# GpSimd's multiplication of the state by C without its wait for the next inject (one layer: GCN, Mamba scan, mixture of experts)

## The chip, the cores and the metric

The kernel runs on one core of a Trainium2 chip. The metric is the device time of one execution in microseconds (us); lower is better. The core has five engines with a queue each: TensorE (PE in the rows; its weight loads are PEld), VectorE (DVE), ScalarE (ACT), GpSimd (POOL) and SyncE (SP), which only issues DMAs here. They run their queues in order and wait for each other on semaphores.

## The reference, cut to what matters

The input x has 8192 rows of 128 values, and adj is a dense 8192 x 8192 matrix. The layer first adds a graph convolution followed by a Mamba block, and then a top-1 mixture of 8 experts.

```python
h = relu(adj @ layernorm(x) @ gcn_w + gcn_b);  h = layernorm(h)
xz = h @ w_in;  xc, z = xz[:, :256], xz[:, 256:]
u = silu(causal_conv4(xc));  dbc = u @ w_xp
dt = softplus(dbc[:, :8] @ w_dt + b_dt);  B = dbc[:, 8:24];  C = dbc[:, 24:]
dA = exp(dt[:, :, None] * A);  dBu = dt[:, :, None] * B[:, None, :] * u[:, :, None]
hst = dA[t] * hst + dBu[t];  ys[t] = hst @ C[t]          # over t, hst is 256 x 16
x = x + ((ys + u * D_skip) * silu(z)) @ w_out
H = gelu(layernorm(x) @ W1 + b1);  p = softmax(H @ Wg + bg);  e = argmax(p)
x = x + p[e] * (H @ Wd[e] + bd[e])
```

The part that the change touches is the sum over the 16 states in `hst @ C[t]`. For each state the kernel makes dA (`decay`), dBu (`inject`), the scan over time (`hidden`), the product with C (`h_c`), and adds that to `y_sum`.

## The kernel before

The 8192 rows are cut into 16 tiles of 512. `body(i)` is a software pipeline, written for every engine: it multiplies the adjacency of tile i+2 (`adjacency`), runs convolution, normalisation, projections and dt of tile i+1 (`front`), the 16 states of tile i (`mamba`), the output product and gating of tile i-1 (`ffn`), the scatter of the rows of tile i-2 to the experts' bins, and a batch of expert work of older tiles (`batch`, `late`). Within a body every engine loops over `s`, the state, from 0 to 15, and all other work is hung into the slot of some s by hand. Nothing but this written order and the semaphores sets what runs when. The data of one state is a 128 x 1024 float32 block: 256 channels as two halves of 128 partitions, 512 time steps each.

What VectorE does in slot s, in order:

- the scan of state s in two halves (line 779). It reads `decay` in SBUF and `inject` in PSUM and writes `hidden[:, s % 2]`.
- in some slots, work of the other stages. Slots 0, 1, 12 and 14 have chains of small instructions; slot 3 has a sum from PSUM and statistics (lines 811 to 819), slot 4 has two products (823, 827), slots 11 and 13 two PSUM reads each (834, 839), slot 7 six convolution steps (872, after the sum below), and slot 15 a cast, four PSUM reads and a product (760, 763, 909).
- the sum `y_sum += h_c` of state s-1 (line 863; lines 848 and 856 are its forms in slots 0 and 1). Both of its inputs are in SBUF. It waits for GpSimd's h_c of state s-1.
- the product `inject = dtu * B` of state s+1 (line 916). Both of its inputs, `dtu_sb` and a row of `bc_ring`, are in SBUF; its output goes to PSUM.

GpSimd makes `h_c[:, s % 2] = hidden[:, s % 2] * C` of state s in one instruction (line 440), both inputs and the output in SBUF, and then issues the indirect DMAs of that slot, which scatter rows, gather rows and weights, or write output (lines 401, 406, 411, 447). ScalarE makes `decay` of state s+1 and keeps the last column of the scan. SyncE loads `bc_ring`, a ring of four states' B and C, and the adjacency ring; its load of state t waits for h_c of state t-4, and later adjacency loads stand behind it on the same queue.

Before h_c of state s, GpSimd waits for three things: the scan of s, the sum of s-2 (it frees `h_c[:, s % 2]`), and `inject` of the next state. `next_state` yields the next state of this tile, after state 15 the first one of the next tile, and nothing where there is no next tile. Nothing in h_c's data depends on that inject.

Of the kernel before, what the change touches and what calls it, by code (L numbers as in the profile page):

```python
# [39 lines left out]
def gnn_mamba_moe(nc, x_rows, x_cols, adj, vecs, consts, sel, gcn_w, w_in, w_xp, w_dt, w_out, W1, Wg, Wd, bd, out):  # L40
# [12 lines left out]
    with ExitStack() as ctx:  # L53
# [131 lines left out]
        def over_halves(ap):  # L185
            return ap.unsqueeze(1).broadcast_to([P, 2, T])
# [19 lines left out]
        def sem(name, per=1):  # L206
            s = ctx.enter_context(nc.semaphore(name))
            PER[name] = per
            return s
# [23 lines left out]
        decay_ready, inject_ready, scan_ready = (  # L233
            sem("decay_ready", SLOTS), sem("inject_ready", SLOTS), sem("scan_ready", SLOTS))
# [55 lines left out]
        def bodies(eng, body):  # L290
            for i in range(-2, 6):
                body(i, i % 2, **stages(i))
            with eng.Fori(6, TILES - 3, 2) as i:
                body(i, 0, **ALL)
                body(i + 1, 1, **ALL)
            for i in range(TILES - 2, TILES + 2):
                body(i, i % 2, **stages(i))
# [4 lines left out]
        def next_state(s, mamba, front):  # L302

            if s + 1 < SLOTS:
                return ((0, s + 1),) if mamba else ()
            return ((1, 0),) if front else ()
# [72 lines left out]
        @block.gpsimd  # L379
        def _(pool):  # L380
            def constant(dst, pattern, base, lanes):
                nc.gpsimd.iota(dst, pattern, base=base, channel_multiplier=lanes,
                               allow_small_or_imprecise_dtypes=True).then_inc(start_c, 1)

            constant(lane[:], [[0, 1]], 0, 1)
            constant(lane8[:], [[0, 1]], 0, EXPERTS)
            constant(need[:], [[0, 1]], EXPERTS, EXPERTS)
            constant(full_at[:], [[0, EXPERTS], [EXPERTS * P, PICKS]], EXPERTS * P, 0)
            constant(some_at[:], [[0, EXPERTS], [EXPERTS * P, PICKS]], EXPERTS, 0)
            constant(offset[:], [[0, EXPERTS], [EXPERTS * P, PICKS]], 0, 0)  # L390
            constant(owner[:], [[P, EXPERTS], [0, PICKS]], 0, 0)
            constant(turn[:], [[1, PICKS], [0, EXPERTS * PICKS]], 1, 0)
            constant(head[:], [[1, EXPERTS]], 0, 0)
            constant(bt_sb[:, 0:P], [[1, P]], 0, 0)
            for q in range(2):
                constant(id_col[:, q], [[P, BLOCKS]], q * T - 2 * T, 1)
            pool.wait_ge(start_v, 1)
            constant(got[0:1, 0, 0, REC - 1:REC], [[0, 1]], 1 << 30, 0)

            def gather_weights(r, j):  # L400
                nc.gpsimd.indirect_dma_start(  # L401
                    out=wd_ring[:, r, j].rearrange("p k c -> p (k c)"), out_offset=None, in_=wd_rows.ap(),
                    in_offset=bass.IndirectOffsetOnAxis(ap=wd_at[:, r, j:j + 1], axis=0)).then_inc(wd_in[r], 16)

            def gather_rows(r, j):
                nc.gpsimd.indirect_dma_start(  # L406
                    out=got[:, r, j], out_offset=None, in_=bins.ap(),
                    in_offset=bass.IndirectOffsetOnAxis(ap=row_at[:, r, j:j + 1], axis=0)).then_inc(row_in[r], 16)

            def scatter_out(r, j):  # L410
                nc.gpsimd.indirect_dma_start(  # L411
                    out=out, out_offset=bass.IndirectOffsetOnAxis(ap=out_at[:, r, j:j + 1], axis=0),
                    in_=o_sb[:, r, j], in_offset=None, bounds_check=N - 1, oob_is_err=False).then_inc(out_in[r], 16)

            def body(i, p, adjacency, front, mamba, ffn, scatter, batch, late):
                c = Count(pool, i)
                q = 1 - p
                for per in (1, 4, 5, 6, 16, 64):
                    c.times_of(per)
                for s in range(SLOTS):  # L420
                    if late and s in OUT_SLOTS:
                        c.wait(o_ready, -5, PICKS + 1)
                    if scatter and s == 1:
                        pool.wait_ge(zero_in, 16 + 16 * FILLS)
                        c.wait(dest_step, -2, 6)
                        c.wait(xn_ready, -2, BLOCKS)
                        c.wait(id_step, -2, 1)
                    if batch and s == 5:
                        pool.wait_ge(table_in, 16 * 2 * EXPERTS)
                        c.wait(ctrl_step, -4, 16)  # L430
                        c.wait(by_done, -6, PICKS)
                    if batch and s == 6:
                        c.wait(scat_in, -2, 16 * BLOCKS)
                        c.wait(o_ready, -6, PICKS + 1)
                    if mamba:
                        c.wait(scan_ready, 0, s + 1)
                        for d, t in next_state(s, mamba, front):
                            c.wait(inject_ready, d, t + 1)
                        c.wait(y_step, 0, s - 1)
                        nc.gpsimd.tensor_tensor(h_c[:, s % 2], hidden[:, s % 2],  # L440
                                                over_halves(bc_ring[:, s % BC_RING, 1]), ALU.mult
                                                ).then_inc(hc_ready, 1)
                    if late and s in OUT_SLOTS:
                        scatter_out(q, OUT_SLOTS.index(s))
                    if scatter and s in (1, 2, 3, 4):
                        b = s - 1
                        nc.gpsimd.indirect_dma_start(  # L447
                            out=bins.ap(), out_offset=bass.IndirectOffsetOnAxis(ap=dest[:, b:b + 1], axis=0),
                            in_=rec[:, p, b], in_offset=None).then_inc(scat_in, 16)
                    if batch and s in (5, 8, 9):  # L450
                        for j in {5: (0, 1), 8: (2,), 9: (3,)}[s]:
                            gather_weights(p, j)
                    if batch and s in (6, 7):
                        for j in (2 * (s - 6), 2 * (s - 6) + 1):
                            gather_rows(p, j)

            bodies(pool, body)
            for f in range(FLUSH):
                k = BATCHES + f
                c = Count(pool, k)  # L460
                c.wait(o_ready, -2, PICKS + 1)
                pool.wait_ge(flush_step, 23 * f + 23)
                c.wait(by_done, -2, PICKS)
                if f == 0:
                    pool.wait_ge(scat_in, 16 * BLOCKS * TILES)
                for j in range(PICKS):
                    gather_rows(k % 2, j)
                for j in range(PICKS):
                    gather_weights(k % 2, j)
                if f:  # L470
                    c.wait(o_ready, -1, PICKS + 1)
                    for j in range(PICKS):
                        scatter_out((k - 1) % 2, j)
            c.wait(o_ready, 0, PICKS + 1)
            for j in range(PICKS):
                scatter_out(k % 2, j)
# [674 lines left out]
```

## Time and profile before

| | us |
|---|---|
| three runs before | 1887.21, 1882.68, 1887.48 |
| median | 1887.21 |
| the profiled execution, its own time | 1887.13 |
| its span, first to last instruction | 1885.3 |
| first scan starts, last h_c starts | 158.2, 1715.4 |

So 1.8 us lie outside the span. The states fill the middle 1557 us, some 97 us for a tile. Ahead of them x is normalised and the first two tiles of the adjacency are multiplied; behind them the experts' remaining batches run. A busy time is the time in which an engine executes; the profile also says, for idle time ahead of an instruction, what ended it. A line in a row is the line of the kernel above.

### The profile page before, as it was taken

To read this page: it belongs to the slowest core of one execution; us is meant where nothing else is said; L and a number is where in the kernel's file an instruction comes from. 1 tells how busy PE (TensorE), PEld (TensorE's weight loads), DVE (VectorE), ACT (ScalarE), POOL (GpSimd) and SP (SyncE) were. 2 spreads that over 40 slices of the span, in tenths; PEclk is the share of its full clock that TensorE was granted. 3 is DMA by queue.
4 is the path that set the end of the run, shared out by engine and by line. 5 is a ranking of instruction groups with operands and counts; after the bars stand their busy time and mean duration, and the time that the engine had idled before them with its cause. 6 is when DMAs were issued, how large, how long until landed. Compare 5 with 4: busy or idle time off the path is not lost. (4 is left out here: it accounts for less than half of the span.)

```text
span 1885.3 us, 18148 instructions
## 1 busy us (share of the span) xinstructions
PE 1534.3 (81%) x4568; PEld 770.3 (41%) x4568; DVE 1557.7 (83%) x2103; ACT 846.2 (45%) x1500; POOL 978.9 (52%) x553
## 2 busy tenths in 40 slices
PE   6799888898989898998989898999899866345554
PEld 2343334444434444444435353544444433223342
DVE  8016999999998999999898989999989999996221
ACT  2033445454446373645464544546363645444211
POOL 0002443545455574747474756666574747586444
PEclk9899998999998999998988999999989886656777
DMA  8899997978776878787787878788868754242232
GB/s 302 296 311 391 379 347 276 328 264 313 260 287 232 307 269 307 261 310 281 274 284 273 283 272 285 270 285 283 270 238 311 260 178 139 94 146 79 82 99 50
DMA packets 155792, 479.52 MB, mean 254 GB/s; under 512 B 19477, under 2 KB 45602, under 8 KB 155698
## 3 DMA queue, kind: packets, MB, share of 16 engines
q1 hardware_dynamic: 139954, 428.59, 64.7%
q0 software_dynamic: 14592, 45.77, 7.5%
q10 hardware_dynamic: 1152, 4.19, 0.6%
q14 instruction: 71, 0.58, 0.1%
q8 instruction: 23, 0.38, 0.1%
HBM read 447.88 MB, written 33.75 MB: 255 GB/s over the span
## 5 line engine op out<-in xcount | busy, mean ns | idle before, releaser
L987 PE MATMUL ps_adj<-ring,nodes 128*128 128x512 f32 x2048 | 964.0, 619 | 86.0 <-DMA ring<-adj 53.5
L440 POOL TENSOR_TENSOR h_c<-hidden,bc_ring 128x1024 f32<-128x1024 f32 x256 | 601.8, 2351 | 783.6 <-DVE inject L916 706.7
L779 DVE TENSOR_TENSOR_SCAN hidden<-decay,state,inject 128x512 f32<-128x512 f32 x512 | 627.6, 1268 | 54.0 <-ACT decay L524 22.9
L987 PEld LDWEIGHTS ps_adj<-ring,nodes 128*128 128x128 f32 x2048 | 397.7, 199 | 610.2 <-issue 481.7
L524 ACT ACTIVATE decay<-dt_sb,negA 128x512 f32<-128x512 f32 x512 | 339.4, 711 | 1.2 <-DVE dt_sb L839 1.0
L916 DVE TENSOR_TENSOR inject<-dtu_sb,bc_ring 128x1024 f32<-128x1024 f32 x256 | 314.4, 1228 | 22.1 <-DMA bc_ring<-bc_dram 14.8
L863 DVE TENSOR_TENSOR y_sum<-y_sum,h_c 128x1024 f32<-128x1024 f32 x224 | 273.5, 1221 | 23.1 <-POOL h_c L440 21.7
L517 ACT COPY state<-hidden 128x2 f32<-128x2 f32 x256 | 49.4, 193 | 535.3 <-DVE hidden L779 534.8
L411 POOL DMA_INDIRECT out<-o_sb,out_at x72 | 85.2, 1183 | 68.3 <-DVE dest L795 22.4
L401 POOL DMA_INDIRECT wd_ring<-wd_rows,wd_at x72 | 105.3, 1462 | 16.6 <-issue 13.6
L406 POOL DMA_INDIRECT got<-bins,row_at x72 | 92.2, 1280 | 18.3 <-issue 16.5
L447 POOL DMA_INDIRECT bins<-rec,dest x64 | 92.6, 1446 | 11.5 <-issue 6.0
L938 PE MATMUL ps_e<-bt_sb,w_sb 128*128 128x512 f32 x128 | 88.0, 825 | 2.3 <-ACT H L629 1.2
L938 PE MATMUL ps_e<-wd_ring,H 128*128 128x128 f32 x512 | 74.1, 292 | 14.7 <-ACT H L629 14.0
L938 PE MATMUL ps_y<-const_sb,rec 128*128 128x128 f32 x128 | 25.1, 357 | 70.1 <-ACT rec L558 70.1
L938 PEld LDWEIGHTS ps_y<-wg_sb,H 128*128 128x128 f32 x512 | 76.6, 240 | 11.0 <-issue 11.0
L938 PE MATMUL ps_f<-u_sb,wxp_sb 128*128 128x512 f32 x64 | 42.1, 793 | 46.4 <-ACT H L597 44.4
L938 PEld LDWEIGHTS ps_e<-wd_ring,H 128*128 128x128 f32 x512 | 69.0, 207 | 22.8 <-ACT H L629 16.5
L938 PE MATMUL ps_y<-wg_sb,H 128*128 128x8 f32 x512 | 77.8, 293 | 0.0
L872 DVE SCALAR_TENSOR_TENSOR u_sb<-conv_in,vec_sb,u_sb 128x512 f32<-128x512 f32 x96 | 65.0, 746 | 11.6 <-ACT u_sb L577 11.6
L938 PE MATMUL ps_e<-const_sb,got 128*128 128x128 f32 x128 | 22.3, 327 | 61.0 <-DMA got<-bins,row_at 59.9
L938 PE MATMUL ps_f<-front_a,win_sb 128*128 128x512 f32 x128 | 69.9, 674 | 0.8 <-ACT conv_in L570 0.8
(166 smaller groups left out, 1360.6 us busy)
## 6 DMA issues: line engine op xcount, KB each, us to landing
ring<-adj SPq DMA_DIRECT2D x512, 512.0 KB, 5.6
bc_ring<-bc_dram SPq DMA_DIRECT2D x256, 512.0 KB, 5.7
bins<-nodes SPq DMA_DIRECT2D x96, 172.0 KB
nodes<-x_rows ACTq DMA_DIRECT2D x8, 512.0 KB, 12.2
x_tile<-x_rows SPq DMA_DIRECT2D x16, 256.0 KB, 5.3
wd_rows<-Wd SPq DMA_DIRECT2D x8, 256.0 KB, 5.0
wd_ring<-wd_rows,wd_at POOLq DMA_INDIRECT x72, 6.3
got<-bins,row_at POOLq DMA_INDIRECT x72, 3.8
```

Source lines behind the costliest of these rows:

```text
L401: nc.gpsimd.indirect_dma_start(out=wd_ring[:, r, j].rearrange("p k c -> p (k c)"), out_offset=None, in_=wd_rows.ap(), in_offset=bass.Indir ...
L406: nc.gpsimd.indirect_dma_start(out=got[:, r, j], out_offset=None, in_=bins.ap(), in_offset=bass.IndirectOffsetOnAxis(ap=row_at[:, r, j:j + ...
L411: nc.gpsimd.indirect_dma_start(out=out, out_offset=bass.IndirectOffsetOnAxis(ap=out_at[:, r, j:j + 1], axis=0), in_=o_sb[:, r, j], in_offs ...
L440: nc.gpsimd.tensor_tensor(h_c[:, s % 2], hidden[:, s % 2], over_halves(bc_ring[:, s % BC_RING, 1]), ALU.mult).then_inc(hc_ready, 1)
L447: nc.gpsimd.indirect_dma_start(out=bins.ap(), out_offset=bass.IndirectOffsetOnAxis(ap=dest[:, b:b + 1], axis=0), in_=rec[:, p, b], in_offs ...
L524: exp = nc.scalar.activation(decay[:, t % 2, h], dt_sb[:, p if d == 0 else q, h], ACT.Exp, scale=negA[:, h, t:t + 1])
L779: scan = nc.vector.tensor_tensor_scan(hidden[:, s % 2, h], decay[:, s % 2, h], inject[:, h], state[:, h, s:s + 1], ALU.mult, ALU.add)
L863: nc.vector.tensor_tensor(y_sum[:], y_sum[:], h_c[:, (s - 1) % 2], ALU.add).then_inc(y_step, 1)
L872: nc.vector.scalar_tensor_tensor(out=u_sb[:, h], in0=conv_in[:, h, k:k + T], scalar=vec("conv_w", TAPS * h + k), in1=u_sb[:, h], op0=ALU.m ...
L916: nc.vector.tensor_tensor(inject[:], dtu_sb[:], over_halves(bc_ring[:, t % BC_RING, 0]), ALU.mult).then_inc(inject_ready, 1)
L938: last = nc.tensor.matmul(dst, stationary, moving, start=(n == 0), stop=(n == len(pairs) - 1))
L987: last = nc.tensor.matmul(ps_adj[:, 0], nodes[:, m], ring[:, g % RING, m % GROUP], start=(m == 0), stop=(m == J - 1))
```

## The change

The two lines that make GpSimd wait for the next inject are taken out. No instruction is added, removed or moved on any engine; lines behind the edit move up by two.

```diff
                     if mamba:
                         c.wait(scan_ready, 0, s + 1)
-                        for d, t in next_state(s, mamba, front):
-                            c.wait(inject_ready, d, t + 1)
                         c.wait(y_step, 0, s - 1)
                         nc.gpsimd.tensor_tensor(h_c[:, s % 2], hidden[:, s % 2],
```

## Rows read from the trace of the kernel before

**Rows 1.** The page, part 1: busy time, share of the span, instructions.

```profile
PE 1534.3 (81%) x4568; PEld 770.3 (41%) x4568; DVE 1557.7 (83%) x2103; ACT 846.2 (45%) x1500; POOL 978.9 (52%) x553
```

**Rows 2.** Busy time in two stretches: length, PE, PEld, DVE, ACT, POOL, granted clock, DMA.

```profile
923.00:1025.00 102.00, 92.56 (x274) 46.89 (x272) 93.61 (x125) 51.03 (x91) 59.30 (x33) 0.90 0.78 269
...
1628.00:1716.00 88.00, 33.85 (x128) 25.08 (x128) 83.16 (x107) 36.24 (x67) 64.72 (x33) 0.60 0.34 111
```

**Rows 3.** The page, part 5: busy us, mean ns, idle before, its releaser.

```profile
L440 POOL TENSOR_TENSOR h_c<-hidden,bc_ring 128x1024 f32<-128x1024 f32 x256 | 601.8, 2351 | 783.6 <-DVE inject L916 706.7
...
L916 DVE TENSOR_TENSOR inject<-dtu_sb,bc_ring 128x1024 f32<-128x1024 f32 x256 | 314.4, 1228 | 22.1 <-DMA bc_ring<-bc_dram 14.8
L863 DVE TENSOR_TENSOR y_sum<-y_sum,h_c 128x1024 f32<-128x1024 f32 x224 | 273.5, 1221 | 23.1 <-POOL h_c L440 21.7
```

**Rows 4.** Timeline, one ordinary state (start us, us, engine): DVE and POOL.

```profile
584.48 2.45 DVE L779 TENSOR_TENSOR_SCAN hidden<-decay,state,inject 128x512 f32<-128x512 f32 x2
584.53 2.34 POOL L440 TENSOR_TENSOR h_c<-hidden,bc_ring 128x1024 f32<-128x1024 f32 x1 [0.42 <-issue]
...
586.90 1.23 DVE L863 TENSOR_TENSOR y_sum<-y_sum,h_c 128x1024 f32<-128x1024 f32 x1
...
588.05 1.23 DVE L916 TENSOR_TENSOR inject<-dtu_sb,bc_ring 128x1024 f32<-128x1024 f32 x1
...
589.41 2.35 POOL L440 TENSOR_TENSOR h_c<-hidden,bc_ring 128x1024 f32<-128x1024 f32 x1 [0.41 <-DVE inject L916]
```

**Rows 5.** Timeline, the last state of the last tile: DVE, then POOL.

```profile
1712.89 2.45 DVE L779 TENSOR_TENSOR_SCAN hidden<-decay,state,inject 128x512 f32<-128x512 f32 x2
1715.31 1.23 DVE L863 TENSOR_TENSOR y_sum<-y_sum,h_c 128x1024 f32<-128x1024 f32 x1
1716.45 2.31 DVE L760 CAST out_at<-got 128x4 uint32<-128x4 f32 x1
1718.67 1.11 DVE L763 SCALAR_TENSOR_TENSOR o_sb<-ps_e,got 128x128 f32<-128x128 f32 x4
```

```profile
1715.42 3.31 POOL L440 TENSOR_TENSOR h_c<-hidden,bc_ring 128x1024 f32<-128x1024 f32 x1
```

**Rows 6.** Queries by line and tile: duration ns as min/median/max, first and last start.

```profile
L440 POOL TENSOR_TENSOR h_c<-hidden,bc_ring x256: 2328/2346/3307, 163.0 to 1715.4; 128x1024 f32<-128x1024 f32 x128
```

```profile
L760 DVE CAST out_at<-got x18: 159/164/2305, 621.3 to 1862.8; 128x4 uint32<-128x4 f32 x18
```

```profile
L779 DVE TENSOR_TENSOR_SCAN hidden<-decay,state,inject x512: 1252/1268/1282, 158.2 to 1714.1; 128x512 f32<-128x512 f32 x171
```

**Rows 7.** Timeline of DVE in one tile: slots 3, 4, 11 and 12.

```profile
841.90 2.45 DVE L779 TENSOR_TENSOR_SCAN hidden<-decay,state,inject 128x512 f32<-128x512 f32 x2
...
846.24 1.19 DVE L863 TENSOR_TENSOR y_sum<-y_sum,h_c 128x1024 f32<-128x1024 f32 x1
...
848.67 2.45 DVE L779 TENSOR_TENSOR_SCAN hidden<-decay,state,inject 128x512 f32<-128x512 f32 x2
...
851.69 1.22 DVE L863 TENSOR_TENSOR y_sum<-y_sum,h_c 128x1024 f32<-128x1024 f32 x1
...
889.01 2.45 DVE L779 TENSOR_TENSOR_SCAN hidden<-decay,state,inject 128x512 f32<-128x512 f32 x2
...
892.68 1.22 DVE L863 TENSOR_TENSOR y_sum<-y_sum,h_c 128x1024 f32<-128x1024 f32 x1
...
898.65 0.18 DVE L879 TENSOR_TENSOR logit<-ps_y,vec_sb 128x32 f32<-128x32 f32 x1
898.87 0.19 DVE L883 TENSOR_REDUCE top<-logit 128x4 f32<-128x32 f32 x1
```

**Rows 8.** Waits: us in total, times, longest.

```profile
DVE hidden L779 <- ACT decay L524: 22.9, 10, 5.0
...
DVE inject L916 <- issue: 5.5, 6, 1.9
DVE hidden L779 <- POOL h_c L440: 5.1, 2, 2.6
```

```profile
SPq L362 <- POOL h_c L440: 490.9, 134, 8.5
```

## The prediction

> **What bounds the kernel now.** I read the busy shares first, then single stretches, then the timeline of one state. Over the whole span VectorE is busy 83% and TensorE 81% [rows 1]; the average hides that the kernel has three parts. In the middle part, where the 16 states of 16 tiles run, VectorE works 93.61 of 102 us and GpSimd 59.30 [rows 2]; most of VectorE's small gaps are the short hand-over ahead of a scan. TensorE is busy 92.56 us there too, and in the last tile, with no adjacency left, only 33.85 of 88 us, while VectorE still works 83.16 of them [rows 2]. So VectorE's own queue sets the pace of the states, with TensorE close behind, and what adds a microsecond between two scans adds it to the end.
>
> Then one state [rows 4]: two scans take 2.45 us, the sum y_sum 1.23, the inject 1.23, and the next scans start; this is a period of 4.9 us without slack. GpSimd's h_c (2.34 us) starts with the scans of the next state, at 584.53, and is over 0.03 us before y_sum starts at 586.90. So h_c always runs under the scans, and never beside y_sum or inject. The change ends exactly this: h_c of state s becomes free to start when scan s ends, which is when VectorE goes on to y_sum and inject.
>
> GpSimd's idle time ahead of h_c is large, 783.6 us, of which 706.7 were ended by inject [rows 3]. It is no cost by itself: GpSimd isn't the bound. What VectorE loses to GpSimd is the wait of y_sum for h_c, 21.7 us in all [rows 3], plus 5.1 us of scans put down to h_c [rows 8]. That is all that an earlier h_c can give back directly.
>
> **What an early h_c costs.** The trace of before holds one instance of the changed kernel. Behind the last state of the last tile there is no next inject, so h_c waited only for its scan [rows 5]. The scans end at 1715.34; y_sum starts at 1715.31 and h_c at 1715.42. y_sum keeps its 1.23 us and ends at 1716.54. h_c takes 3.31 us instead of the median 2.346 [rows 5, 6]: it stood still until y_sum was over and then ran, 1716.54 to 1718.73. VectorE's next instruction, a cast of 128x4 values, took 2305 ns where its median is 164 [rows 6]: it began before y_sum had ended and yet finished only with h_c. So the two engines exclude each other here, the one that is ahead goes first, and at the hand-over GpSimd wins against a VectorE instruction that is already queued. The price for VectorE is 2305 - 164 = 2.14 us.
>
> Which instructions take part? The scans don't: all 512 lie between 1252 and 1282 ns although nearly all run beside h_c [rows 6], and they read one SBUF tensor, write SBUF and take inject from PSUM. y_sum reads two SBUF tensors and did hold up h_c. Inject reads two as well. That inject will itself be held up by a running h_c is my inference, since the held instruction of the trace is a cast with one input. The Trainium skill says it outright (SBUF — State Buffer, Who interferes with whom): a VectorE instruction with two SBUF inputs and a GpSimd instruction that reads SBUF exclude each other for the whole instruction, and whichever issues first goes first. The trace agrees for y_sum against h_c (3.31 us for 2.35); for inject against h_c no row of before shows it.
>
> **The sum, slot by slot of a full tile.** No queue is reordered and no DMA moved; only the start of h_c, and with it the indirect DMAs behind it, come earlier by up to one y_sum and one inject.
> - Slots 2, 5 to 10, 14 and 15 have y_sum straight behind the scans. y_sum goes first, h_c next, and the instruction after y_sum (inject, the convolution, a small product or the cast) is held 2.14 us. Slots 0 and 1 have chains of small instructions ahead of y_sum, some with two SBUF inputs; h_c is ready 0.08 us behind the scan's end and takes over after the first of them, for about the same 2.14. These are 11 slots, 23.5 us.
> - In slot 3 the work ahead of y_sum reads PSUM or one tensor and can run beside h_c. h_c would run from 0.08 to 2.43 us behind the scan's end, and y_sum used to start at 846.24 - 844.35 = 1.89 [rows 7]: held 0.5 us, or 0.9 if the small tensor_scalar there is held; I take 0.8. Slot 4: y_sum used to start 851.69 - 851.12 = 0.57 behind the scan; held 1.7 to 1.9, I take 1.7. Slot 11: 892.68 - 891.46 = 1.22, held 1.2; slot 13 has the same shape, 1.2. In slot 12 the two instructions behind y_sum (0.18 and 0.19 us) have at most one SBUF tensor and a vector, and run beside h_c [rows 7]: 2.14 less 0.37, 1.8.
> - Together 23.5 + 0.8 + 1.7 + 1.2 + 1.2 + 1.8 = 30.2 us a tile, and 16 x 30.2 = 483 us.
>
> Against it stands what goes. y_sum's waits for h_c, 21.7 us, vanish, since h_c of s-1 is over before scan s. VectorE's waits for others shrink as VectorE itself becomes later: 22.9 us of scans on decay, 5.5 us of inject behind the logits, 5.1 us on h_c, 33.5 us in all [rows 8]. TensorE has some 92 us of work for a tile that now lasts about 127, so I let all of these go. SyncE's queue waits 490.9 us for h_c [rows 8], with adjacency loads behind it; it will wait longer, but in step with VectorE, so it costs TensorE time it no longer needs.
>
> The profiled execution took 1887.13 us, as good as the median of 1887.21. 1887.1 + 483 - 21.7 - 33.5 = 2315 us.
>
> **Its own range.** Low end: if only instructions over 0.5 us are held and the small chains run beside h_c, slots 0, 1, 14 and 15 lose 0.6 to 1.6 us of their price each, about 4 us a tile, 65 us in all: 2250. If h_c also sometimes falls under waits that stay, some 20 less, 2230. High end: the other waits stay (+33), and each of the 11 hits costs a whole h_c of 2.35 instead of 2.14 (+37): 2385; a TensorE whose granted clock sinks as it idles more (0.60 in the last tile against 0.90 [rows 2]) could lengthen the chains through TensorE and ScalarE: 2400. Below nothing the cost can't go in this case, since VectorE is the bound in every tile and 483 us is twenty times what is given back.
>
> **The rivals.**
> - *Inject keeps the port* (no change). y_sum and inject are back to back and of one kind, while the trace's held instruction was a cast. If VectorE passes from one to the other without letting go, h_c stands still through both and then runs under the next scans, exactly as before. The sum is the old one: h_c of about 4.8 us, 1887 us, within 0.3%. For it: two instructions of VectorE overlap in the rows by some 0.09 us. Against it: the cast overlapped y_sum by the same 0.09 (1716.45 against 1716.54) and lost.
> - *No exclusion of inject, and the gain comes* (faster). If only y_sum holds up h_c, and inject, which writes PSUM, runs beside it, then h_c is over 2.35 us behind y_sum, well before the next y_sum. y_sum's 21.7 us and the scans' 5.1 go: 1887.1 - 26.8 = 1860; TensorE, nearly as busy, would take a part of it back, so 1865. It decides itself on whether inject stays at 1228 ns with h_c beside it. Against it: y_sum and inject have the same kinds of inputs, and the held cast has fewer.
> - *Held in some slots only.* Who wins at y_sum's end may turn on a few tens of ns and come out differently in even and odd bodies. Half of the hits would give about 2090; 1900 to 2230.
> - *The wait was idle.* That the change does nothing because h_c waits for something else is excluded: 706.7 us of idle time end with inject [rows 3].
>
> **How the numbers follow.** The full hold-up has 0.76, the port kept by inject 0.08, the gain 0.06, some slots only 0.08, above 2400 us 0.02. The forecast is 2315 us. 2230 to 2400 holds the first case; down to 2120 it takes in about half of the partial one, near 0.8 in all. About 0.3% is what a measurement of this kernel can tell from no change: faster by more 0.06, within 0.08, slower by more 0.76 + 0.08 + 0.02 = 0.86.
>
> **What would show it.** Inject's mean rises from 1228 to about 2.9 to 3.4 us, h_c's from 2351 to some 3.2, while y_sum stays near 1221 and the scans at 1268. VectorE's busy time rises by about 450 us, as held time counts as busy. An ordinary state takes 7.0 us from scan to scan instead of 4.9, a tile about 127 us, and y_sum's wait for h_c is gone. Inject at 1228 ns with h_c in y_sum's shadow would make the prediction wrong on its second step; h_c at 4.8 us would prove the first rival.

## The result and the profile after

The changed kernel takes 2306.43 us (median of four runs, 2304.65 to 2309.28) against 1886.7 us (median of four runs of the kernel before); the ratio is 1.2229, 95% interval 1.2204 to 1.2254. It is slower by 420 us. The profiled execution took 2304.65 us, its span is 2302.8.

The page of the changed kernel, parts 1 and 5 (busy us, mean ns, idle before, releaser; lines behind the edit are two lower than in the rows of before):

```profile
PE 1598.0 (69%) x4568; PEld 803.1 (35%) x4568; DVE 2023.7 (88%) x2103; ACT 848.0 (37%) x1500; POOL 1121.2 (49%) x553
...
L438 POOL TENSOR_TENSOR h_c<-hidden,bc_ring 128x1024 f32<-128x1024 f32 x256 | 749.1, 2926 | 1059.3 <-DVE hidden L777 1045.6
...
L777 DVE TENSOR_TENSOR_SCAN hidden<-decay,state,inject 128x512 f32<-128x512 f32 x512 | 627.6, 1267 | 33.4 <-issue 9.8
...
L914 DVE TENSOR_TENSOR inject<-dtu_sb,bc_ring 128x1024 f32<-128x1024 f32 x256 | 537.1, 2098 | 16.5 <-DMA bc_ring<-bc_dram 14.7
...
L861 DVE TENSOR_TENSOR y_sum<-y_sum,h_c 128x1024 f32<-128x1024 f32 x224 | 328.2, 1465 | 0.0
```

The number of instructions is that of [rows 1], but VectorE is busy 2023.7 us where it was 1557.7: 466.0 us more for the same work. Its idle time in the span fell from 327.6 to 279.1 us. The two together are the 417.5 us between the spans. Against [rows 3], inject grew from 1228 to 2098 ns on average, y_sum from 1221 to 1465, h_c from 2351 to 2926; the scans kept their 1267. y_sum waits for h_c no longer.

One ordinary state (slot 5) in the timeline, first VectorE, then GpSimd:

```profile
1054.24 1.20 DVE L861 TENSOR_TENSOR y_sum<-y_sum,h_c 128x1024 f32<-128x1024 f32 x1
1055.36 3.38 DVE L914 TENSOR_TENSOR inject<-dtu_sb,bc_ring 128x1024 f32<-128x1024 f32 x1
1058.84 2.45 DVE L777 TENSOR_TENSOR_SCAN hidden<-decay,state,inject 128x512 f32<-128x512 f32 x2
```

```profile
1054.42 3.24 POOL L438 TENSOR_TENSOR h_c<-hidden,bc_ring 128x1024 f32<-128x1024 f32 x1 [2.89 <-DVE hidden L777]
1057.81 1.81 POOL L401 DMA_INDIRECT wd_ring<-wd_rows,wd_at  x1 [0.15 <-issue]
1059.93 0.96 POOL L401 DMA_INDIRECT wd_ring<-wd_rows,wd_at  x1 [0.30 <-issue]
```

This is [rows 5] repeated: y_sum is first, h_c stands until it ends at 1055.44 and runs to 1057.66, and inject, queued at 1055.36, ends 1.08 us behind h_c. Where other work stands behind the scans, another instruction is hit. VectorE in slots 0, 1, 3, 4 and 11 of the same tile:

```profile
1014.30 1.99 DVE L793 CAST dest<-dest_f 128x4 uint32<-128x4 f32 x1
...
1022.74 2.40 DVE L699 TENSOR_TENSOR has<-rem,full_at 128x32 f32<-128x32 f32 x1
...
1041.12 0.93 DVE L815 TENSOR_SCALAR rec<-rec 128x4 f32<-128x4 f32 x1
...
1047.69 2.95 DVE L861 TENSOR_TENSOR y_sum<-y_sum,h_c 128x1024 f32<-128x1024 f32 x1
...
1101.20 2.30 DVE L861 TENSOR_TENSOR y_sum<-y_sum,h_c 128x1024 f32<-128x1024 f32 x1
```

Instructions of some 0.2 us take 2 us because h_c is running: the product `has` (2.40 us for 0.19) with two inputs in SBUF, but also two instructions with one, the cast in slot 0 and the tensor_scalar at 1041.12 (0.93 us for 0.17). In every slot of every tile one instruction is held.

### The profile page after: what moved, and what is told of

The parts are those of the page before. It is cut to its first block and busy times, and to the rows that moved or that the text cites. A ratio compares the mean times of both kernels' runs of the same rounds, so it can differ in the third digit from the quotient of the medians.

```text
span 2302.8 us, 18078 instructions
## 1 busy us (share of the span) xinstructions
PE 1598.0 (69%) x4568; PEld 803.1 (35%) x4568; DVE 2023.7 (88%) x2103; ACT 848.0 (37%) x1500; POOL 1121.2 (49%) x553
## 5 line engine op out<-in xcount | busy, mean ns | idle before, releaser
L438 POOL TENSOR_TENSOR h_c<-hidden,bc_ring 128x1024 f32<-128x1024 f32 x256 | 749.1, 2926 | 1059.3 <-DVE hidden L777 1045.6
L985 PEld LDWEIGHTS ps_adj<-ring,nodes 128*128 128x128 f32 x2048 | 407.2, 203 | 633.5 <-issue 534.1
L914 DVE TENSOR_TENSOR inject<-dtu_sb,bc_ring 128x1024 f32<-128x1024 f32 x256 | 537.1, 2098 | 16.5 <-DMA bc_ring<-bc_dram 14.7
L861 DVE TENSOR_TENSOR y_sum<-y_sum,h_c 128x1024 f32<-128x1024 f32 x224 | 328.2, 1465 | 0.0
L936 PE MATMUL ps_f<-u_sb,wxp_sb 128*128 128x512 f32 x64 | 58.1, 1061 | 112.2 <-ACT H L595 101.7
L411 POOL DMA_INDIRECT out<-o_sb,out_at x72 | 100.2, 1391 | 68.2 <-DVE o_sb L761 23.5
L870 DVE SCALAR_TENSOR_TENSOR u_sb<-conv_in,vec_sb,u_sb 128x512 f32<-128x512 f32 x96 | 96.4, 1069 | 11.5 <-ACT u_sb L575 11.5
L936 PEld LDWEIGHTS ps_y<-const_sb,rec 128*128 128x128 f32 x128 | 28.5, 328 | 192.9 <-ACT rec L556 192.9
L406 POOL DMA_INDIRECT got<-bins,row_at x72 | 83.3, 1157 | 18.2 <-issue 16.5
L936 PE MATMUL ps_f<-front_a,win_sb 128*128 128x512 f32 x128 | 78.5, 747 | 6.8 <-ACT conv_in L568 3.9
```

Of the source, the lines that this page charges most:

```text
L406: nc.gpsimd.indirect_dma_start(out=got[:, r, j], out_offset=None, in_=bins.ap(), in_offset=bass.IndirectOffsetOnAxis(ap=row_at[:, r, j:j + ...
L411: nc.gpsimd.indirect_dma_start(out=out, out_offset=bass.IndirectOffsetOnAxis(ap=out_at[:, r, j:j + 1], axis=0), in_=o_sb[:, r, j], in_offs ...
L438: nc.gpsimd.tensor_tensor(h_c[:, s % 2], hidden[:, s % 2], over_halves(bc_ring[:, s % BC_RING, 1]), ALU.mult).then_inc(hc_ready, 1)
L861: nc.vector.tensor_tensor(y_sum[:], y_sum[:], h_c[:, (s - 1) % 2], ALU.add).then_inc(y_step, 1)
L870: nc.vector.scalar_tensor_tensor(out=u_sb[:, h], in0=conv_in[:, h, k:k + T], scalar=vec("conv_w", TAPS * h + k), in1=u_sb[:, h], op0=ALU.m ...
L914: nc.vector.tensor_tensor(inject[:], dtu_sb[:], over_halves(bc_ring[:, t % BC_RING, 0]), ALU.mult).then_inc(inject_ready, 1)
```

## Experiments

The theory: h_c and those instructions of VectorE that read two inputs from SBUF exclude each other, whoever is first goes first, and the turn changes at the end of an instruction. "The port" stands here for whatever the two exclude each other on; the runs show the exclusion and its price, not the wire. The rivals: any overlap or any access to memory costs, or the loss comes from the rest of the pipeline. The kernel before ran beside each group of runs on the same chip, so its median differs a little between them.

### Inject with one input in SBUF

```diff
+            nc.vector.memset(inject[:], 1.0)
...
-                        nc.vector.tensor_tensor(inject[:], dtu_sb[:], over_halves(bc_ring[:, t % BC_RING, 0]),
+                        nc.vector.tensor_tensor(inject[:], dtu_sb[:], inject[:],
```

> The changed kernel, but inject is dtu times its own old value in PSUM instead of dtu times B, so it reads one SBUF tensor where it read two; the product with B is left out and the output is another one. Theory (an instruction of VectorE with two SBUF inputs and h_c exclude each other): inject falls from 3.38 us to about 1.23 us in slots 2, 5, 6, 8, 9 and 10, where it stands behind y_sum, and runs beside h_c; y_sum still goes first, so h_c stays at about 3.24 us there; the holds in the ten other slots stay. 2306 less 6 x 2.15 x 16 = 206 gives about 2100 us. Rival (what costs is the hand-over behind y_sum or writing to memory beside h_c, whatever is read): inject stays at 3.38 us and the time at 2306.

One execution, 2103.32 us (the kernel before beside it 1888.85). From the groups by line:

```profile
L862 DVE TENSOR_TENSOR y_sum<-y_sum,h_c 128x1024 f32<-128x1024 f32 x224 | 328.2, 1465 | 0.0
L915 DVE TENSOR_TENSOR inject<-dtu_sb,inject 128x1024 f32<-128x1024 f32 x256 | 312.6, 1221 | 15.8 <-DMA bc_ring<-bc_dram 14.0 <-DVE dtu_sb L908 1.5
```

Inject is back at 1221 ns, 1212 to 1230 in all 256, of which 90 lie wholly inside a running h_c, and y_sum is held as before. The time is the expected 2100 within 4 us. Same columns, same output in PSUM, same place in the queue: the second SBUF input is what makes inject collide. This is the step that the trace of before did not show.

### GpSimd writes and doesn't read

```diff
-                        nc.gpsimd.tensor_tensor(h_c[:, s % 2], hidden[:, s % 2],
-                                                over_halves(bc_ring[:, s % BC_RING, 1]), ALU.mult
-                                                ).then_inc(hc_ready, 1)
+                        nc.gpsimd.tensor_tensor(h_c[:, s % 2, 0, 0:1], hidden[:, s % 2, 0, 0:1],
+                                                bc_ring[:, s % BC_RING, 1, 0:1], ALU.mult)
+                        nc.gpsimd.memset(h_c[:, s % 2, 0, 1:T], 0.25)
+                        nc.gpsimd.memset(h_c[:, s % 2, 1], 0.5).then_inc(hc_ready, 1)
```

> The changed kernel, but GpSimd's product is left out: it multiplies one column (which carries the waits) and fills the rest of h_c by two memsets, which write SBUF and read nothing. Theory (h_c's reads through the second read port of VectorE collide): inject back at 1.23 us and y_sum at 1.2 us in every slot, the casts at 0.16 us or a little above if they need the write port, time 1850 to 1890 us. Rival (any access of GpSimd to SBUF excludes VectorE's two-input instructions): what follows y_sum is held for the length of the memsets in each of 16 slots, some 0.5 to 2 us each, 2000 us or more.

One execution, 1856.34 us. VectorE, then GpSimd, in slots 14 and 15:

```profile
897.20 0.18 DVE L888 SCALAR_TENSOR_TENSOR pick<-logit,vec_sb 128x32 f32<-128x32 f32 x1
...
897.69 0.19 DVE L900 TENSOR_TENSOR pick_bf<-vec_sb,top 128x32 bf16<-128x32 f32 x1
897.83 1.23 DVE L915 TENSOR_TENSOR inject<-dtu_sb,bc_ring 128x1024 f32<-128x1024 f32 x1
...
902.64 1.07 DVE L759 CAST out_at<-got 128x4 uint32<-128x4 f32 x1
```

```profile
897.27 0.52 POOL L440 MEMSET h_c<- 128x511 f32 x1
897.73 0.52 POOL L441 MEMSET h_c<- 128x512 f32 x1
901.68 1.08 POOL L438 TENSOR_TENSOR h_c<-hidden,bc_ring 128x1 f32<-128x1 f32 x1 [3.44 <-DVE hidden L778]
902.71 0.52 POOL L440 MEMSET h_c<- 128x511 f32 x1
903.16 0.52 POOL L441 MEMSET h_c<- 128x512 f32 x1
```

`pick_bf` and inject, with two SBUF inputs each, begin while a memset runs and take their usual 0.19 and 1.23 us, and the memsets their 0.52. `pick`, which h_c held for 2.3 us, takes 0.18; it began just ahead of the first memset, so it shows less. The one-column product of 0.18 us takes 1.08, since y_sum holds it up.

The loss is gone, as the theory said, and with y_sum's waits for h_c gone as well the kernel is under the one before. The time alone doesn't show that the reads were the cause, since the memsets are also shorter and in pieces (about 1 us in all against 2.35); the rows do, and the copies in the same three pieces, further down, which read and do collide.

The cast takes 1.07 us for 0.16: it collides with writes too. It ended with the second memset, at 903.71 against 903.68, and so in all twelve such casts; it got no turn between the two, and why no run shows. So there are two kinds of collision, and nearly all of the 420 us is of the read kind.

### h_c told of the sum instead of the inject

```diff
                         c.wait(scan_ready, 0, s + 1)
-                        c.wait(y_step, 0, s - 1)
+                        c.wait(y_step, 0, s)
```

> The changed kernel with one index changed: h_c of state s waits for the sum y_sum of state s-1 instead of that of s-2. So it is told to start about when inject has just begun, one instruction earlier than in the kernel before. Theory (whoever is first keeps the port, and GpSimd only wins at the end of an instruction if it already waits): inject goes first in slots 1 to 6, 8 to 11 and 13 and stays at 1.23 us, h_c there takes about 3.4 us and costs nothing, since it then runs under the scans; in slots 0, 7, 12, 14 and 15 other two-input instructions or a cast stand between the sum and inject, and h_c takes the port there, about 2.15 + 2.15 + 1.9 + 1.7 + 1.15 = 9.1 us a tile, 145 us; 1980 to 2020 us in all. Rival (every overlap of h_c with y_sum or inject costs a whole h_c): 2306 us as in the changed kernel.

2013.59 us in two runs, ratio 1.0665, interval 1.0563 to 1.0768: inside the expected 1980 to 2020, but the two runs are 16 us apart (2005.71 and 2021.46), and the rows below are of the faster. Slot 14, where small instructions stand ahead of inject, and slot 1, where inject follows at once; VectorE, then GpSimd:

```profile
860.59 2.13 DVE L899 TENSOR_TENSOR pick_bf<-vec_sb,top 128x32 bf16<-128x32 f32 x1
...
888.48 1.23 DVE L914 TENSOR_TENSOR inject<-dtu_sb,bc_ring 128x1024 f32<-128x1024 f32 x1
```

```profile
860.32 2.35 POOL L438 TENSOR_TENSOR h_c<-hidden,bc_ring 128x1024 f32<-128x1024 f32 x1 [4.89 <-DVE y_sum L861]
...
888.72 3.19 POOL L438 TENSOR_TENSOR h_c<-hidden,bc_ring 128x1024 f32<-128x1024 f32 x1 [5.92 <-DVE y_sum L854]
```

In slot 1 inject began 0.24 us ahead of h_c and kept its 1.23 us; h_c stood 0.85 us and then ran under the scans, at no cost. In slot 14 h_c came first and the next product paid 1.9 us. So overlap by itself costs nothing; the order of arrival decides who pays, and only VectorE's payments reach the end. In three tiles slot 13 paid too, 1.3 to 2.2 us: there inject began only 0.22 to 1.11 us after y_sum had ended, and h_c got in between.

### The wait taken out in six slots alone

```diff
+                        if s not in (2, 5, 6, 8, 9, 10):
                             for d, t in next_state(s, mamba, front):
                                 c.wait(inject_ready, d, t + 1)
```

> The kernel before with the wait taken out in slots 2, 5, 6, 8, 9 and 10 alone. Theory (the held time of each slot is local and goes to the end one to one): inject 3.38 us in these six slots and 1.23 us in the others; 6 x 2.15 x 16 = 206 us more, less y_sum's waits of 21 us and up to 33 us of other waits: 2040 to 2075 us. Rival (a part of the loss comes from the rest of the pipeline, such as TensorE's clock or SyncE's queue, and appears only with all slots, or half a change is as bad as the whole): under 2000 or over 2150.

1938.71 us in two runs, ratio 1.0269, interval 1.023 to 1.0308. This is 50 us over the kernel before beside it, not the 150 to 190 that the theory asked for. The time lies in the rival's range (under 2000), so the rows have to say whether the rest of the pipeline is the reason. VectorE, then GpSimd, in slots 6 and 10 of one tile:

```profile
899.26 1.20 DVE L864 TENSOR_TENSOR y_sum<-y_sum,h_c 128x1024 f32<-128x1024 f32 x1
900.38 1.23 DVE L917 TENSOR_TENSOR inject<-dtu_sb,bc_ring 128x1024 f32<-128x1024 f32 x1
...
924.35 1.20 DVE L864 TENSOR_TENSOR y_sum<-y_sum,h_c 128x1024 f32<-128x1024 f32 x1
925.47 3.38 DVE L917 TENSOR_TENSOR inject<-dtu_sb,bc_ring 128x1024 f32<-128x1024 f32 x1
```

```profile
900.47 1.96 POOL L401 DMA_INDIRECT wd_ring<-wd_rows,wd_at  x1 [0.30 <-issue]
902.59 2.35 POOL L441 TENSOR_TENSOR h_c<-hidden,bc_ring 128x1024 f32<-128x1024 f32 x1 [0.16 <-issue]
...
925.27 2.49 POOL L441 TENSOR_TENSOR h_c<-hidden,bc_ring 128x1024 f32<-128x1024 f32 x1
```

In slot 6 GpSimd still issued the indirect DMAs of the slot ahead when y_sum ended, so h_c came too late to stand in inject's way. The lateness is handed on: h_c of slot 4, which still waits for inject, ran under the scans of slot 5, the DMA behind it made h_c of slot 5 run under the scans of slot 6, and that one's two DMAs kept GpSimd until 902.43. The rival's reason does not show in the rows: those of the six slots that have no hit take what they took before (4.80 to 4.84 us, slot 9 5.75). The first two tiles, which have no indirect DMAs yet, are hit in all six slots, the next two, which only scatter rows, in slots 6, 8, 9 and 10, and from the fifth on only slot 10 is hit (once slot 9 too). These are 33 hits instead of 96, and VectorE is busy 1625.2 us, 67.5 more than before. The price of a hit is the same 2.15 us; what I had wrong is that a slot can be counted without looking at what GpSimd does just before.

### The wait taken out in slots 14 and 15 alone

The edit is the one above with `s not in (14, 15)`, again in the kernel before. It tests the corrected theory in two slots with no indirect DMA ahead.

> The kernel before with the wait taken out in slots 14 and 15 alone. The run with six slots showed the hold in slot 10 only, where GpSimd was on time; in the others the h_c ahead ran under the scans and an indirect DMA behind it made GpSimd late, so that the next h_c came after inject had begun. Slots 14 and 15 have no indirect DMA ahead of them. Theory (the hold comes wherever GpSimd already waits when y_sum ends): the small product behind y_sum in slot 14 and the cast in slot 15 take 2.3 us instead of 0.19 and 0.16 us, 2 x 2.15 x 16 = 69 us less up to 25 us of other waits: 1930 to 1957 us. Rival (with h_c of the neighbouring slots still waiting, no hold comes, and slot 10 was an exception): within 5 us of the kernel before.

1948.64 us in five runs, ratio 1.0377, interval 1.0338 to 1.0415, inside the expected 1930 to 1957. The two instructions behind y_sum, by line:

```profile
L890 DVE SCALAR_TENSOR_TENSOR pick<-logit,vec_sb 128x32 f32<-128x32 f32 x16 | 35.3, 2208 | 0.0
...
L761 DVE CAST out_at<-got 128x4 uint32<-128x4 f32 x18 | 29.3, 1627 | 8.2 <-DMA got<-bins,row_at 8.2
```

Both slots are hit in all 16 tiles. Two slots with GpSimd on time cost 67 us, more than six of which it mostly missed.

### GpSimd copies instead of multiplying

```diff
-                        nc.gpsimd.tensor_tensor(h_c[:, s % 2], hidden[:, s % 2],
-                                                over_halves(bc_ring[:, s % BC_RING, 1]), ALU.mult
-                                                ).then_inc(hc_ready, 1)
+                        nc.gpsimd.tensor_tensor(h_c[:, s % 2, 0, 0:1], hidden[:, s % 2, 0, 0:1],
+                                                bc_ring[:, s % BC_RING, 1, 0:1], ALU.mult)
+                        nc.gpsimd.tensor_copy(h_c[:, s % 2, 0, 1:T], hidden[:, s % 2, 0, 1:T])
+                        nc.gpsimd.tensor_copy(h_c[:, s % 2, 1], hidden[:, s % 2, 1]).then_inc(hc_ready, 1)
```

> The changed kernel, but GpSimd's product is left out: it multiplies one column (which carries the waits) and copies the rest of hidden to h_c, so it reads one SBUF tensor and writes one. Theory (any read of GpSimd needs the shared port): y_sum holds the copy up, and the instruction behind y_sum is held for about as long as the copy then runs, in all 16 slots as in the changed kernel; if the copy takes 1 to 2 us alone, 0.8 to 1.9 us of hold in slots 2, 5, 6, 8, 9 and 10, and 2000 to 2230 us in all. Rival (only the second input of GpSimd's product collides): no holds, 1850 to 1890 us.

One execution, 1910.44 us, 29 us over the kernel before beside it: between the two expectations (2000 to 2230, and 1850 to 1890), and in neither. VectorE, then GpSimd, in an ordinary slot, and VectorE behind the small instructions of slot 14:

```profile
866.39 1.20 DVE L862 TENSOR_TENSOR y_sum<-y_sum,h_c 128x1024 f32<-128x1024 f32 x1
867.50 1.23 DVE L915 TENSOR_TENSOR inject<-dtu_sb,bc_ring 128x1024 f32<-128x1024 f32 x1
...
922.05 1.67 DVE L915 TENSOR_TENSOR inject<-dtu_sb,bc_ring 128x1024 f32<-128x1024 f32 x1
```

```profile
866.56 1.07 POOL L438 TENSOR_TENSOR h_c<-hidden,bc_ring 128x1 f32<-128x1 f32 x1 [1.76 <-DVE hidden L778]
867.58 1.61 POOL L440 COPY h_c<-hidden 128x511 f32<-128x511 f32 x1
869.14 0.61 POOL L441 COPY h_c<-hidden 128x512 f32<-128x512 f32 x1
...
921.47 0.61 POOL L440 COPY h_c<-hidden 128x511 f32<-128x511 f32 x1
922.02 0.61 POOL L441 COPY h_c<-hidden 128x512 f32<-128x512 f32 x1
```

A copy, with one input, does collide: 1.61 us behind inject where it takes 0.61 alone, and inject takes 1.67 where a copy was first. A memset in the same place took its usual 0.52 us behind inject. That much of the theory holds. My number was wrong because the work of GpSimd is now in three instructions: by the rows the one-column product has its turn at the end of y_sum and is over at once, inject gets in, and the copies wait behind it. The port is passed on with each instruction that reads.

### h_c in two halves

```diff
-                        nc.gpsimd.tensor_tensor(h_c[:, s % 2], hidden[:, s % 2],
-                                                over_halves(bc_ring[:, s % BC_RING, 1]), ALU.mult
-                                                ).then_inc(hc_ready, 1)
+                        for h in range(2):
+                            half = nc.gpsimd.tensor_tensor(h_c[:, s % 2, h], hidden[:, s % 2, h],
+                                                           bc_ring[:, s % BC_RING, 1], ALU.mult)
+                        half.then_inc(hc_ready, 1)
```

> The changed kernel with h_c made by two instructions of 512 columns instead of one of 1024. Theory (the port is given instruction by instruction, and a waiting engine gets it at the end of the other's instruction): inject is held only by the first half, some 1.0 us instead of 2.15, and the second half waits for inject; in slots 2, 5, 6, 8, 9 and 10 this saves 1.1 x 6 x 16 = 105 us, while in the other slots VectorE's next two-input instruction is held by the second half and nothing is saved: 2190 to 2225 us. Rival (GpSimd keeps the port from one instruction to its next): inject at 3.4 us and 2306 us.

2156.14 us in two runs, ratio 1.1435, interval 1.1391 to 1.1478. VectorE in slot 8:

```profile
1013.73 1.20 DVE L862 TENSOR_TENSOR y_sum<-y_sum,h_c 128x1024 f32<-128x1024 f32 x1
1014.85 2.30 DVE L915 TENSOR_TENSOR inject<-dtu_sb,bc_ring 128x1024 f32<-128x1024 f32 x1
```

Inject is held 1.07 us instead of 2.15: by the first half only. The same product, cut in two, costs 150 us less than in one piece, more than the 105 expected, and the time is below the expected 2190 to 2225. Besides the 1.08 us in five of the six slots, slot 6 loses nothing now (4.80 us from scan to scan), since GpSimd, busier by the hand-overs, comes late there as in the run with six slots; slots 14 and 15 save 0.4 and 0.9 us; slot 7 pays 0.5 us more.

### Indirect DMAs placed elsewhere

These two runs keep every wait of the kernel before and go after its own 21.7 us of y_sum waiting for h_c [rows 3], nearly all of which stand in slots 7 and 9, behind two indirect DMAs each. First placing:

```diff
-                    if batch and s in (5, 8, 9):
-                        for j in {5: (0, 1), 8: (2,), 9: (3,)}[s]:
+                    if batch and s in (5, 7, 8, 9):
+                        for j in {5: (0,), 7: (1,), 8: (2,), 9: (3,)}[s]:
...
-                    if batch and s in (6, 7):
-                        for j in (2 * (s - 6), 2 * (s - 6) + 1):
+                    if batch and s == 6:
+                        for j in range(PICKS):
```

> The kernel before, every wait kept, but GpSimd's gathers of a batch lie elsewhere: one weight gather in slot 5 instead of two, the four row gathers all in slot 6 (whose h_c is followed by the long slot 7), one weight gather in slot 7. Theory (y_sum waits for h_c in slots 7 and 9 because two indirect DMAs ahead make GpSimd late, by 0.87 us and 0.84 us): these 21.7 us of waits go, 1862 to 1872 us. Rival (TensorE or a wait for a later landing takes the gain): 1880 us or more.

1870.27 us in twelve runs against 1881.48, ratio 0.9954, interval 0.9929 to 0.9979. The time is in the expected 1862 to 1872, but the kernel before was faster on this chip too, and the gain is about half of the 21.7 us. The waits of VectorE:

```profile
DVE y_sum L863 <- POOL h_c L440: 14.6, 17, 3.4
```

Slot 9 no longer waits and slot 7 in only four of the tiles with gathers (0.5 to 1.5 us), but slot 8 now does, 0.68 us in nearly every tile with gathers and 3.4 in the last, because the four gathers, which begin behind slot 7's scans, last longer than slot 7. Second placing:

```diff
-OUT_SLOTS = (0, 10, 11, 12)
+OUT_SLOTS = (0, 11, 12, 13)
...
-                    if batch and s in (5, 8, 9):
-                        for j in {5: (0, 1), 8: (2,), 9: (3,)}[s]:
+                    if batch and s in (5, 8, 9, 10):
+                        for j in {5: (0,), 8: (1,), 9: (2,), 10: (3,)}[s]:
...
-                        for j in (2 * (s - 6), 2 * (s - 6) + 1):
+                        for j in {6: (0, 1, 2), 7: (3,)}[s]:
```

> The kernel before, every wait kept, with GpSimd's indirect DMAs placed once more: weight gathers one each in slots 5, 8, 9 and 10, three row gathers in slot 6 and the fourth in slot 7, output scatters in slots 0, 11, 12 and 13. So no slot but 6 has two. Theory (y_sum waits for h_c only where GpSimd has more indirect DMAs ahead than fit before the next inject ends; four in slot 6 were one too many): y_sum's wait for h_c falls from 21.7 us to under 3 us and the ratio to the kernel before is 0.985 to 0.992. Rival (TensorE is the bound behind it): no better than the first placing, 0.995.

1871.08 us in ten runs against 1886.48, ratio 0.9919, interval 0.989 to 0.9947. From the waits of VectorE:

```profile
DVE hidden L779 <- ACT decay L524: 21.5, 10, 4.7
...
DVE hidden L779 <- POOL h_c L440: 8.4, 3, 3.1
...
DVE y_sum L863 <- POOL h_c L440: 5.9, 7, 2.1
```

y_sum's wait for h_c fell from 21.7 to 5.9 us, not to the expected 3. The time is 0.5 to 1.1% under that of the kernel before, an interval that excludes no change, just inside the expected 0.985 to 0.992. The rows are of an execution of 1880.23 us, the second longest of the ten (1858.64 to 1881.05), so the median may have less waiting. The waits left in them stand mostly around slot 13 and are no smaller than the 22.9 us of before [rows 8]; how much of the gain the rival (TensorE is the bound behind it) takes is open.

## Why the prediction was right

**The bound.** VectorE's queue set the pace before and does now: what was added between two scans came out at the end, 466.0 us of held time less 48.5 us of idle time, 417.5 us of span. TensorE's granted clock fell meanwhile, from 0.885 to 0.825 on average, and its idle time grew from 351 to 705 us, but VectorE waited less than before, so nothing of this shows at the end.

**The price of a hit.** 2.14 us, taken from one cast in the last tile [rows 5, 6], was right: an ordinary state went from 4.83 to 6.96 us. The trace of before held the changed kernel once, in the one place where `next_state` yields nothing.

**Inject collides.** This was inferred from y_sum and from the Trainium skill (SBUF — State Buffer, Who interferes with whom); the changed kernel's 3.38 us and the run with one input show it.

**The sum.** 30.2 us a tile were predicted. From scan to scan in an ordinary tile, slot by slot: 1.8 in slot 0, 2.1 in slot 1, 2.1 in each of 2, 5, 6, 8, 10, 14 and 15, 0.8 in slot 3, 1.7 in slot 4, 1.1 each in 11 and 13, 1.7 in slot 12, and in 7 and 9 some 2.0 once the vanished waits of 0.87 and 0.84 us are added back. Added before rounding that makes 29.2 us, and 16 x 29.2 = 467 against 483. Most of the overshoot is in slots 0, 11, 12 and 13. In slot 0 one small product came ahead of h_c and a reduction ran beside it, so that only the cast behind them was held.

**What goes.** Predicted 55.2 us of waits, measured 48.5 us of idle time. All of the 55.2 went, and 6.6 us came in: scans that wait for nothing the profile shows ("issue") stand at 9.8 us instead of 3.2. TensorE waits longer now, at no cost.

**What was wrong in it.** The signs that I gave for the changed profile did not follow from my own list. It holds inject in six slots of 16 only, which makes its mean 1228 + 6/16 x 2150 = 2034 ns, near the measured 2098; I wrote 2.9 to 3.4 us. The rest of the 2098 are the first tiles and the last, where the work of other stages is missing and inject is hit in more slots, 104 times in all. The same holds for y_sum, which I said would stay near 1221 although slots 4, 11 and 13 hold it, and for h_c (2926, not 3.2 us). The 483 us were also called twenty times what is given back; against the 55.2 us of the same sum they are nine times. The 2.14 us were also counted as a property of the slot. In the changed kernel that gave the right number, since h_c is early everywhere; the run with six slots shows that it is a property of what GpSimd does just before.

**The rivals.** Inject does not keep the port: VectorE's two products are back to back, and h_c still gets in between, in every tile. That inject doesn't collide is excluded by its 3.38 us. A loss in some slots only didn't come here, where h_c was early in all 256; it came in the runs in which GpSimd was late in some slots or was told later.

## What to carry to other kernels

A wait that no data needs may be what keeps two engines off a shared port: before it is taken out, look at what the waiting instruction would then run beside, and what both read and write in SBUF. In this kernel VectorE's instructions with two inputs in SBUF were held by a GpSimd that read, and so were a cast and a tensor_scalar with one. The last or first turn of a loop, where such a wait is absent, can show the price in the trace at hand. When the engine that sets the pace can be held, order so that it arrives first; an instruction of the other engine then costs it nothing (inject kept its 1.23 us in the run told of the sum). Where it can't, cutting the other's instruction in two halved the hold here (1.07 us for 2.15).

## What the runs showed of the hardware that I had not expected

- GpSimd's memsets, which read nothing, hold a cast of VectorE (1.07 us for 0.16), but not products with two SBUF inputs (inject at 1.22 to 1.23 us with a memset inside it, 103 times).
- The port is passed on with each instruction that reads, in both directions: a one-column product of GpSimd of 0.18 us is enough to have had its turn, and VectorE's next instruction follows. With memsets it isn't: a cast that was queued ahead of two of them ended only with the second, in twelve of twelve.
- GpSimd's indirect DMAs seem to need the port as well when they start. In the changed kernel's slot 5 the first takes 1.81 us and the next 0.96; the first began 0.93 us before inject was over. Of the 280 indirect DMAs of this trace the 144 that start with no large two-input product running take 0.94 to 1.06 us; the 136 others take what is left of that product and 0.82 to 0.91 us more, save one (1.01). The trace of before has the same, with 165 and 115. This is read from the traces; no run isolates it.
